# Expert rows added to token rows by indirect transfers, semaphores cleared inside other stages, slabs stored by partition

## The chip, the cores and the metric

The kernel runs on one NeuronCore of a Trainium2 chip, as one program. The metric is the device time of one execution in microseconds (us). The core's engines are PE (TensorE, matrix products and transposes), DVE (VectorE), ACT (ScalarE), POOL (GpSimd) and SP (SyncE, which only issues transfers and waits); PEld is the loading of weights into PE. Transfers between DRAM and the on-chip memory are issued from the queues of SP, ACT and POOL and are carried out by 16 DMA engines that all queues share.

## What is computed

Two blocks, each a graph convolution followed by a feed-forward part, on x of 16 items x 512 nodes x 16 channels x 12 times. Seen as tokens, an item is 192 rows (one per channel and time) of 512 values, so there are 3072 token rows.

```python
x = x + L0_conv(ln_c(x))
t = to_tokens(x);  t = t + L0_ffn(ln_t(t));  x = from_tokens(t)   # mixture of experts
x = x + L1_conv(ln_c(x))
t = to_tokens(x);  t = t + L1_ffn(ln_t(t));  x = from_tokens(t)   # ternary weights, 8-bit activations

def L0_ffn(x):                       # E = 8 experts, cap = 1.25 * N * 2 / E = 960 rows each
    gate = softmax(x @ Wr.T)         # N = 3072 token rows of H = 512
    top2_val, top2_idx = top_k(gate, 2)
    # first choices of all tokens, then second choices, are ranked within their expert;
    # an assignment ranked over cap gets weight 0
    y_e = (silu(x @ Wg[e].T) * (x @ Wu[e].T)) @ Wd[e].T
    return sum_e comb[:, e] * y_e    # comb: the kept gate values
```

## The kernel before, in words

The program is a row of stages. Each stage is one block of code in which every engine has its own instruction stream; engines are ordered by semaphores (a wait is `wait_ge(sem, value)`), and at the end of a block all engines meet before the next block begins. Nothing of a stage overlaps the next one. The stages in order are: constants; `normalise` n0 (layer norm of x over nodes, item by item); `conv_weights`; the channel attention c0; `mix_channels`; the time attention t0; `graph_conv` g0, which writes x1; `normalise` n1, which also keeps the unnormalised token rows in DRAM (`raw_rows`) and computes the router's logits; `route`; `experts`; `combine`; `conv_weights`, c1, mixing, t1 and `graph_conv` g1 of the second block; `quantise_weights`; `feed_forward`.

Item order inside a stage is software pipelined by hand: `turns` calls `turn(b, q, i)` for each item b with q = b mod 2 naming the buffer, and one turn holds parts of item b, b+1 and b+2 (`third`, `second`, `first`). `ready(n)` and `free(n, depth)` are the semaphore values for "n is done" and "the buffer that n will use is free".

**Slabs.** x, x1, x2 and x3 lie in DRAM as [item, node, channel x time]; a slab of an item is loaded into 128 partitions of 4 x 192 values, that is 512 runs of 768 bytes.

**Semaphores.** Each stage makes its own. `Semaphores.clear` sets all that were made since the last call back to zero in a block of its own, by one SP instruction each (L119), and frees them. It is called after g0 and after `quantise_weights`.

**route** finds for each token its two experts and its place (slot) in each. Slot numbers go into `s.slots`, gate values into `s.gates`, and a table of which token sits in each of 64 tiles of 120 slots is made by products of one-hot matrices on PE (L1073) and two DVE steps (L1149, L1150).

**experts** handles 8 experts of 8 tiles of 120 rows. POOL gathers the rows of the tiles ahead (`x_xin`, L1221), PE transposes them (`ex_t`), and PE computes gate and up products (`ex_g`, `ex_u`) and the down product (`ex_d`), each as three passes of high and low parts. ACT copies `ex_d` out of PSUM (`x_yo`, L1396, two buffers) and stores it to `y_slots` in DRAM (L1398).

**combine** ("join") then goes item by item: SP loads the raw rows (L1459), POOL gathers four times 96 rows of `y_slots` (L1482; two halves of an item x two choices), DVE adds the four with their gate values (L1506), takes statistics (L1522, L1523 and the four small steps of `node_stats`, L254 to L260), POOL raises to the power -0.5 (L1488), DVE makes the shift `L_nm` (L266), ACT normalises into `L_xnT` (L1580) and copies `L_xa` out of PSUM (L1570), PE transposes both (L1544), DVE copies the transposed rows into `L_shared` (L1529), SP stores `xn_rows`, ACT stores x2 (L1573). Raw rows have two buffers. At its start ACT's queue issues the 13 loads of the next convolution's weights (`conv_loads`, L167).

## Time and profile before

| what | value |
|---|---|
| runs shown | 1921.21, 1924.47 and 3712.32 us; median 1924.47 us |
| profiled execution, its own time | 1922.03 us |
| its span, first to last instruction | 1920.2 us |
| busy shares of the span | PE 75%, DVE 61%, ACT 39%, POOL 28% |
| mean granted TensorE clock | 0.854 of full |
| DRAM traffic | 192.4 MB, mean 100 GB/s |

Reading it: the span is what the trace covers; 1.8 us of the execution lie outside it. The third run is nearly double the other two and is left out of every comparison below. Since the stages follow one another with a meeting of all engines between them, the shares of the whole say little: each stage has its own limit, and the time of the kernel is the sum of the stages'. By the first and last instructions of each in the trace, the long ones are g0 and g1 (313 us and 315 us), experts (434 us), feed_forward (258 us), combine (148 us), n1 (94 us), n0 (86 us) and route (59 us); c1 takes 15 us.

### The profile page before, as it was taken

Reading aid. Unit: us, or ns where it says so; the run is one execution under the profiler, and the core shown is the slowest. Engines: PE = TensorE matmul, PEld = TensorE weight load, DVE = VectorE, ACT = ScalarE, POOL = GpSimd, SP = SyncE. Lnnn points to the kernel's source line nnn. Section 1 sums busy time; section 2 is a strip of 40 time slices with the busy share of each in tenths; the row PEclk is TensorE's granted clock in tenths of the full one; section 3 lists DMA queues with packets and bytes.
Section 4 is the critical chain, followed back from the end, with each engine's and each line's share of the span. In section 5 each row is a group of like instructions: output and inputs, shape, how many; then the busy total and the mean of one; then the engine's idle time right before and its main releaser. Section 6 shows DMA issues by size and latency. Waiting matters only on the chain. (4 is left out here: it accounts for less than half of the span.)

```text
span 1920.2 us, 28801 instructions
## 1 busy us (share of the span) xinstructions
PE 1432.1 (75%) x8462; PEld 1174.9 (61%) x8462; DVE 1163.3 (61%) x2466; ACT 746.6 (39%) x1181; POOL 532.3 (28%) x854
## 2 busy tenths in 40 slices
PE   4577999997462499999999533487999994177776
PEld 3466788886241388888888423385888883145554
DVE  4622588887366555444444267522688886588886
ACT  2412455553241133333333122222555552077765
POOL 1100155566111311111110256200255665011111
PEclk7678999998696599999999755587999997588988
DMA  6432022222472133344441587343122221112221
GB/s 194 139 89 76 17 67 73 61 70 66 140 229 84 46 113 115 120 121 122 127 127 42 157 241 243 118 132 121 35 73 60 71 74 49 34 57 74 83 89 58
DMA packets 152117, 192.42 MB, mean 100 GB/s; under 512 B 11737, under 2 KB 103417, under 8 KB 152061
## 3 DMA queue, kind: packets, MB, share of 16 engines
q1 hardware_dynamic: 118061, 129.16, 22.7%
q10 hardware_dynamic: 24784, 34.24, 6.0%
q0 software_dynamic: 9216, 28.32, 4.9%
q8 instruction: 29, 0.48, 0.1%
q14 instruction: 27, 0.22, 0.0%
HBM read 125.63 MB, written 66.06 MB: 100 GB/s over the span
## 5 line engine op out<-in xcount | busy, mean ns | idle before, releaser
L724 PE MATMUL g_y<-L_z,L_pt 128*128 128x192 f32 x1024 | 195.8, 335 | 1.5 <-ACT L_pt L937 0.5
L724 PEld LDWEIGHTS g_y<-L_z,L_pt 128*128 128x128 f32 x1024 | 165.6, 192 | 6.8 <-ACT L_pt L937 6.8
L882 POOL TENSOR_TENSOR L_xr<-L_xr,L_lnb 128x192 f32<-128x192 f32 x128 | 105.6, 853 | 204.5 <-DMA L_xr<-x 108.5
L1221 POOL DMA_INDIRECT x_xin<-xn_rows,x_index x64 | 64.2, 1003 | 298.2 <-PE ex_t L1235 150.5
L929 ACT ACTIVATE L_e<-g_s,L_nm 128x512 f32<-128x512 f32 x128 | 88.0, 687 | 78.7 <-DVE L_nm L770 77.5
L692 PE MATMUL g_z<-L_kw,L_xnT 96*128 96x192 f32 x512 | 96.8, 344 | 26.1 <-DVE L_v L800 26.1
L692 PEld LDWEIGHTS g_z<-L_kw,L_xnT 96*128 96x128 f32 x512 | 87.1, 198 | 38.2 <-DVE L_v L800 38.2
L1315 DVE TENSOR_TENSOR x_mid<-ex_g,x_sig 128x480 f32<-128x480 f32 (+1 forms) x48 | 31.4, 654 | 122.5 <-ACT x_sig L1390 122.5
L770 DVE TENSOR_REDUCE L_nm<-g_s 128x1 f32<-128x512 f32 x128 | 87.5, 684 | 25.4 <-PE g_s L701 24.6
L779 DVE SCALAR_TENSOR_TENSOR L_p<-L_e,L_rl,L_adj 128x512 f32<-128x512 f32 x128 | 99.1, 774 | 4.7 <-DVE L_rl L777 0.3
L1368 ACT ACTIVATE x_xh<-ex_t 128x480 fp32r<-128x480 f32 x64 | 36.6, 572 | 160.1 <-PE ex_t L1235 151.8
L937 ACT ACTIVATE L_pt<-g_t 128x512 f32<-128x512 f32 x128 | 75.8, 593 | 45.6 <-PE g_t L709 45.4
L889 POOL TENSOR_TENSOR L_t<-L_rstd 128x48 f32<-128x48 f32 x96 | 29.2, 304 | 222.4 <-DVE L_rstd L824 217.3
L709 PE MATMUL g_t<-s_ident,L_p 128*128 128x128 f32 x512 | 77.4, 274 | 9.6 <-DVE L_p L779 9.6
L1745 PE MATMUL ff_u<-s_wup,ff_q1s 128*96 128x512 bf16 x256 | 79.0, 464 | 5.4 <-DVE ff_q1s L1830 4.0
L899 POOL TENSOR_TENSOR L_d<-L_d,L_lng 128x192 f32<-128x192 f32 x128 | 73.1, 602 | 35.7 <-DVE L_d L830 35.7
L709 PEld LDWEIGHTS g_t<-s_ident,L_p 128*128 128x128 f32 x512 | 63.2, 140 | 30.4 <-DVE L_p L779 25.2
L720 PEld LDWEIGHTS g_y<-L_res,L_xnT 97*128 97x128 f32 x512 | 75.4, 193 | 6.2 <-ACT L_y L943 1.1
L1249 PE MATMUL ex_g<-x_xh,x_guh 128*128 128x480 f32 (+1 forms) x192 | 76.9, 400 | 3.1 <-DVE x_gul L1306 3.1
L320 PE MATMUL n_psx<-s_ident,L_xa 128*96 128x128 f32 x256 | 45.3, 338 | 43.4 <-DMA L_xa<-x 28.7
L1263 PE MATMUL ex_d<-x_wdh,x_hh 128*120 128x512 f32 (+1 forms) x192 | 77.7, 404 | 0.0
L720 PE MATMUL g_y<-L_res,L_xnT 97*128 97x96 f32 x512 | 75.5, 270 | 0.5 <-ACT L_y L943 0.5
(273 smaller groups left out, 3791.9 us busy)
## 6 DMA issues: line engine op xcount, KB each, us to landing
xn_rows<-L_xnT SPq DMA_DIRECT2D x48, 384.0 KB, 3.7
L_xnT<-xn_rows SPq DMA_DIRECT2D x48, 384.0 KB, 3.4
y_slots<-x_yo ACTq DMA_DIRECT2D x64, 240.0 KB, 2.4
x<-L_y SPq DMA_DIRECT2D x32, 384.0 KB, 2.7
L_xa<-in_x SPq DMA_DIRECT2D x16, 384.0 KB, 4.0
L_raw<-xn_rows SPq DMA_DIRECT2D x16, 384.0 KB, 3.4
L_xr<-in_x SPq DMA_DIRECT2D x16, 384.0 KB, 3.8
L_xa<-x SPq DMA_DIRECT2D x16, 384.0 KB, 4.1
```

Source lines behind the costliest of these rows:

```text
L692: last = nc.tensor.matmul(psz[:, k // 2, CT * (k % 2):CT * (k % 2) + CT], xnT[q][0:HALF, h, P * k:P * k + P], kw[q][0:HALF, h, NPROJ:], st ...
L709: last = nc.tensor.transpose(pst[k % 2][:, P * c:P * c + P], pr[k % 2][:, P * c:P * c + P], s.ident[:, :])
L720: nc.tensor.matmul(out[:, HALF * h:HALF * h + HALF], xnT[q][0:HALF + 1, h, P * k:P * k + P], s.res[0:HALF + 1, h, :], start=(h == 0), stop ...
L724: last = nc.tensor.matmul(out, pt[k % 2][:, P * c:P * c + P], z[q][:, c, :], start=False, stop=(c == NK - 1))
L770: nc.vector.tensor_reduce(s.nm2[:, k % 2:k % 2 + 1], pss[k % 2][:, :], AX, ALU.max, negate=True).then_inc(nmax_done, 1)
L779: nc.vector.scalar_tensor_tensor(out=pr[k % 2][:, :], in0=e[k % 2][:, :], scalar=s.rl[:, k % 2:k % 2 + 1], in1=s.adj[:, k, :], op0=ALU.mul ...
L882: last = nc.gpsimd.tensor_tensor(v_, v_, gain(s.lnb), ALU.add)
L929: nc.scalar.activation(e[k % 2][:, :], pss[k % 2][:, :], ACT.Exp, bias=s.nm2[:, k % 2:k % 2 + 1], accum_out=s.l[:, k % 2:k % 2 + 1]).then_ ...
L937: nc.scalar.activation(pt[k % 2][:, :], pst[k % 2][:, :], ACT.Copy).then_inc(probs_turned_sb, 1)
L1249: last = nc.tensor.matmul(ps_[z][0:size, 0:SN], w[:, k, off + at:off + at + size], x[q][:, k, SN * c:SN * c + SN], start=(k == 0 and x is ...
L1263: last = nc.tensor.matmul(psd[t % 2][0:ST, :], h[0:size, j, ST * t:ST * t + ST], w[0:size, j, :], start=(j == 0 and h is hh and w is wdh), ...
L1745: last = nc.tensor.matmul(psu[0:HALF, c, :], q1s[q][:, k, HALF * h:HALF * h + HALF], wup[:, k, 512 * c:512 * c + 512], start=(k == 0), sto ...
```

## The change

Four things change.

1. **Expert rows are added in DRAM.** `raw_rows` becomes the first 3072 rows of a tensor `sums`, with 960 spare rows behind them. `experts` multiplies a tile by its gate values while it leaves PSUM (ACT, scale from `x_gate`), and POOL adds it into `sums` with an indirect transfer whose destination rows come from a table and which adds to what is there. Unused slots go to spare rows. The gate values are gathered by POOL, 120 values of 4 bytes per tile, from a small DRAM tensor `gate_rows` that `route` writes. Output tiles get four buffers in place of two. An expert's additions start only when all of the expert before have landed. `y_slots`, `s.slots`, the gathers of `combine` and its weighted sums are gone.
2. **combine is written anew** around loads of `sums`: raw rows have four buffers, all four are loaded at the start, and SP issues the stores of x2 as well.
3. **Semaphores are cleared inside other stages**: by SP in `experts` (those of the stages before it) and in the attention c1. The two blocks of `clear` are gone.
4. **Slabs are stored by partition**: x, x1, x2, x3 lie as [item, partition, 4 x 192], one run of 3072 bytes per partition. The host lays x out so; the output keeps the old form.

`route` also makes two more tables (where a slot's gate value lies, and to which row it is added), with a third block of columns in the one-hot product.

Of the diff stand here the new parts and what they replace; the removed gathers and weighted sums of `combine` are those of the function above.

```diff
-    def clear(self):
-        with self.nc.Block() as block:
-            @block.sync
-            def _(sp):
-                for sem in self.live:
-                    sp.sem_clear(sem)
-        self.ctx.close()
-        self.live = []
+    def retire(self):
+        self.old, self.retired, self.live, self.ctx = self.live, self.ctx, [], ExitStack()
+    def clear_retired(self, sp):
+        for sem in self.old:
+            sp.sem_clear(sem)
+    def reuse(self):
+        self.retired.close()
...
+                if clear:
+                    s.sems.clear_retired(sp)
...
+                sp.wait_ge(gated, 2)
+                for c in range(2):
+                    at = TOKENS * (c + 1)
+                    sp.dma_start(gate_rows[at:at + TOKENS, :].rearrange("(p j) o -> p (j o)", j=TILES),
+                                 s.gates[:, c, :]).then_inc(gates_out, 16)
+                sp.wait_ge(gates_out, 32)
...
+                for c in range(2):
+                    act.wait_ge(hots, 2 * c + 1)
+                    nc.scalar.activation(col_tok[c][:, :, 2, :], col_hot[c][:, :, :], ACT.Copy,
+                                         scale=float(c + 1)).then_inc(hots_kind, 1)
...
-                        last = nc.tensor.matmul(pst[0:ST, 0:2 * ST_TILES], row_hot[c][:, j, :],
+                        last = nc.tensor.matmul(pst[0:ST, 0:3 * ST_TILES], row_hot[c][:, j, :],
...
-                step(V.tensor_copy(low[:, :], pst[0:ST, 0:ST_TILES]))
-                V.scalar_tensor_tensor(out=s.table[:, :], in0=pst[0:ST, ST_TILES:2 * ST_TILES], scalar=float(TOKEN_BASE),
-                                       in1=low[:, :], op0=ALU.mult, op1=ALU.add).then_inc(tabled, 1)
-                dve.wait_ge(tabled, 1)
+                step(V.tensor_copy(made[:, :], pst[0:ST, 0:3 * ST_TILES]))
+                part, tile, kind = (made[:, ST_TILES * n:ST_TILES * n + ST_TILES] for n in range(3))
+                step(V.scalar_tensor_tensor(out=token[:, :], in0=tile, scalar=float(HALF), in1=part,
+                                            op0=ALU.mult, op1=ALU.add))
+                V.tensor_copy(s.table[:, 0, :], token[:, :]).then_inc(tabled, 1)
+                step(V.scalar_tensor_tensor(out=gate_at[:, :], in0=part, scalar=float(TILES), in1=tile,
+                                            op0=ALU.mult, op1=ALU.add))
+                V.scalar_tensor_tensor(out=s.table[:, 1, :], in0=kind, scalar=float(TOKENS), in1=gate_at[:, :],
+                                       op0=ALU.mult, op1=ALU.add).then_inc(tabled, 1)
+                step(V.scalar_tensor_tensor(out=spare[:, :], in0=kind, scalar=0.0, in1=spare[:, :],
+                                            op0=ALU.is_equal, op1=ALU.mult))
+                V.tensor_tensor(s.table[:, 2, :], token[:, :], spare[:, :], ALU.add).then_inc(tabled, 1)
+                dve.wait_ge(tabled, 3)
...
+                s.sems.clear_retired(sp)
...
+                def gather(e, ts):
+                    pool.wait_ge(index_done, ready(e))
+                    for t in ts:
+                        n = e * EST + t
+                        if n >= 4:
+                            pool.wait_ge(turned, ready(n - 4))
+                        nc.gpsimd.indirect_dma_start(xin[t % 4][:, :], None, tokens,
+                                                     row(index[e % 2][:, t:t + 1])).then_inc(x_in[t % 4], 16)
+                def gather_gates(e):
+                    pool.wait_ge(places_done, ready(e))
+                    for t in range(EST):
+                        nc.gpsimd.indirect_dma_start(gate[e % 2][:, t:t + 1], None, gate_rows,
+                                                     row(places[e % 2][:, 0, t:t + 1])).then_inc(gates_in, 16)
+                def scatter(e, ts):
+                    if ts is early and e > 0:
+                        for j in range(4):
+                            pool.wait_ge(sent[j], scattered(e))
+                    for t in ts:
+                        pool.wait_ge(y_sb, ready(e * EST + t))
+                        nc.gpsimd.indirect_dma_start(sums, row(places[e % 2][:, 1, t:t + 1]), yo[t % 4][:, :], None,
+                                                     compute_op=ALU.add).then_inc(sent[t % 4], 16)
+                early, late = range(EST // 2), range(EST // 2, EST)
+                gather(0, early)
+                gather(0, late)
+                gather(1, early)
+                for e in range(E):
+                    gather_gates(e)
+                    if e + 1 < E:
+                        gather(e + 1, late)
+                    scatter(e, early)
+                    if e + 2 < E:
+                        gather(e + 2, early)
+                    scatter(e, late)
+                for j in range(4):
+                    pool.wait_ge(sent[j], scattered(E))
...
+                            if n == 3 and ahead:
+                                for j in range(4) if reused else ():
+                                    dve.wait_ge(sent[j], scattered(e))
+                                copy_places(e + 1, r)
...
-                def send(e, t):
+                def send(e, q, t, reused):
                     n = e * EST + t
+                    if t == 0:
+                        act.wait_ge(gates_in, (e + 1) * (16 * EST))
                     act.wait_ge(down_done, ready(n))
-                    act.wait_ge(sent[t % 2], dma_free(e * (EST // 2) + t // 2))
-                    nc.scalar.activation(yo[t % 2][:, :], psd[t % 2][0:ST, :], ACT.Copy).then_inc(y_sb, 1)
-                    act.wait_ge(y_sb, ready(n))
-                    act.dma_start(ys[n], yo[t % 2][:, :]).then_inc(sent[t % 2], 16)
-                def turn(e, q, here=True, ahead=True):
+                    if reused or t >= 4:
+                        act.wait_ge(sent[t % 4], scattered(e) + t // 4 * 16)
+                    nc.scalar.activation(yo[t % 4][:, :], psd[t % 2][0:ST, :], ACT.Identity,
+                                         scale=gate[q][:, t:t + 1]).then_inc(y_sb, 1)
...
+        raw = [(half(s.raw0, 0), half(s.raw0, 1)), (half(s.raw1, 0), half(s.raw1, 1)),
+               (s.e0[0:HALF, :], s.e1[0:HALF, :]), (s.p0[0:HALF, :], s.p1[0:HALF, :])]
+        xnT, x2 = [s.xnT0, s.xnT1], [s.xa0, s.xa1]
...
+                def load(b, z):
+                    sp.wait_ge(xn_done, free(b, 4))
+                    sp.wait_ge(raw_turned, free(b, 4))
+                    for h in range(2):
+                        sp.dma_start(raw[z][h], raw_rows[b][:, h, :]).then_inc(row_in[z], 16)
+                def store(b, r):
+                    sp.wait_ge(xn_done, ready(b))
+                    sp.dma_start(xn_rows[b], xnT[r][0:HALF, :, :]).then_inc(sent[r], 16)
+                    sp.wait_ge(x_sb, ready(b))
+                    sp.dma_start(x_nodes[b], x2[r][:, :, :]).then_inc(kept[r], 16)
+                for b in range(4):
+                    load(b, b)
+                store(0, 0)
+                store(1, 1)
+                with sp.Fori(0, B // 4 - 1) as i:
+                    for z in range(4):
+                        load(i * 4 + z + 4, z)
+                        store(i * 4 + z + 2, z % 2)
+                store(B - 2, 0)
+                store(B - 1, 1)
...
+                def statistics(b, z, i):
+                    step.begin(b * STAT_STEPS)
+                    dve.wait_ge(row_in[z], (i + 1) * 32)
+                    nc.vector.bn_stats(s.bst[0:HALF, 0, :], raw[z][0])
+                    step(nc.vector.bn_stats(s.bst[0:HALF, 1, :], raw[z][1]))
+                    node_stats(nc, s, step, z % 2, eps).then_inc(var_done, 1)
...
+                def apply_norm(b, z, stores):
+                    r = z % 2
+                    act.wait_ge(shift_done, ready(b))
+                    act.wait_ge(back_turned, free(b, 2))
+                    act.wait_ge(sent[r], stores * 16)
+                    for h in range(2):
+                        last = nc.scalar.activation(half(xnT[r], h), raw[z][h], ACT.Identity,
+                                                    bias=s.nm[0:HALF, r, h:h + 1], scale=s.rs[0:HALF, r, h:h + 1])
+                    last.then_inc(xn_done, 1)
+                def copy_x(b, z, stores):
+                    r = z % 2
+                    act.wait_ge(raw_turned, ready(b))
+                    act.wait_ge(kept[r], stores * 16)
+                    nc.scalar.activation(x2[r][:, :, :].rearrange("p (a k) x -> p a (k x)", a=2),
+                                         psx[r][:, :, 0:2 * CT], ACT.Copy).then_inc(x_sb, 1)
...
+    by_partition = lambda a: a.rearrange("b p (k x) -> b p k x", k=NK)
...
-    xn_rows, raw_rows = dram("xn_rows", [TOKENS, N]), dram("raw_rows", [TOKENS, N])
-    x1, x2, x3 = (dram(n, [B, N, CT]) for n in ("x1", "x2", "x3"))
-    y_slots = dram("y_slots", [SLOTS + 1, N])
+    xn_rows, sums = dram("xn_rows", [TOKENS, N]), dram("sums", [TOKENS + EST * ST, N])
+    raw_rows = sums[0:TOKENS, :]
+    x1, x2, x3 = (dram(n, [B, P, NK * CT]) for n in ("x1", "x2", "x3"))
+    gate_rows = dram("gate_rows", [3 * TOKENS, 1])
...
-            s.sems.clear()
-            normalise(nc, s, "n1", node_major(x1), 1e-5, rows(xn_rows), keep=rows(raw_rows))
+            graph_conv(nc, s, "g0", rows(xn_rows), by_partition(d["x"]), by_partition(x1))
...
+                s.sems.retire()
+                small_attention(nc, s, "c1", True, clear=True)
+                s.sems.reuse()
+                (ternary,) = s.sems("loads2", "ternary")
...
-            s.sems.clear()
-            feed_forward(nc, s, node_major(x3), node_major(out))
+            feed_forward(nc, s, by_partition(x3), node_major(out))
...
-    d["x"] = a["x"].transpose(0, 1, 3, 2).reshape(B, N, CT)
+    slabs = a["x"].transpose(0, 1, 3, 2).reshape(B, NK, P, CT)
+    d["x"] = slabs.transpose(0, 2, 1, 3).reshape(B, P, NK * CT)
```

How the change moves instructions, at three places.

**SP, from the end of g0 into n1.** Before: `L_y` is the last slab of g0, the row at L119 is the clearing.

```order
L622 DMA L_xr<-in_x 128x4x192
L626 DMA x<-L_y 128x4x192 x2
L608 UNCONDITIONAL_BRANCH
L116 UNCONDITIONAL_BRANCH
L119 ISA x83
L115 UNCONDITIONAL_BRANCH
L288 UNCONDITIONAL_BRANCH
L297 DMA L_xa<-x 128x4x192 x2
```

The same place of the changed kernel:

```order
L629 DMA L_xr<-in_x 128x768
L633 DMA x<-L_y 128x768 x2
L615 UNCONDITIONAL_BRANCH
L290 UNCONDITIONAL_BRANCH
L299 DMA L_xa<-x 128x768 x2
L242 UNCONDITIONAL_BRANCH
```

The block with 83 clearings is gone; the loads of n1 follow the last stores with one block boundary between.

**POOL, experts.** Before, a loop over pairs of experts whose body is 16 of these gathers, each behind a step of a register; its beginning:

```order
L1027 UNCONDITIONAL_BRANCH
L1206 UNCONDITIONAL_BRANCH
L1213 UNCONDITIONAL_BRANCH
L1215 ISA
L1221 DMA x_xin<-xn_rows,x_index 120x512
L1217 REGISTER_ALU
```

The changed kernel, from the start of the stage to the second expert's additions (`x_gate` gate values, `sums` the additions of `x_yo`):

```order
L1244 UNCONDITIONAL_BRANCH
L1254 DMA x_xin<-xn_rows,x_index 120x512 x12
L1260 DMA x_gate<-gate_rows,x_places 120x1 x8
L1254 DMA x_xin<-xn_rows,x_index 120x512 x4
L1269 DMA sums<-x_yo,x_places 4032x512 x4
L1254 DMA x_xin<-xn_rows,x_index 120x512 x4
L1269 DMA sums<-x_yo,x_places 4032x512 x4
L1260 DMA x_gate<-gate_rows,x_places 120x1 x8
L1254 DMA x_xin<-xn_rows,x_index 120x512 x4
```

Per expert POOL now issues 8 gathers of rows, 8 of gate values and 8 additions, where it issued 8 gathers of rows.

**DVE, combine, one item.** Before, first item (the loop's turns hold the same, with the copies of `cb_wgt` and `cb_idx` behind):

```order
L1506 SCALAR_TENSOR_TENSOR L_raw<-L_e,cb_wgt,L_raw 96x512
L1506 SCALAR_TENSOR_TENSOR L_raw<-L_p,cb_wgt,L_raw 96x512
L1506 SCALAR_TENSOR_TENSOR L_raw<-L_e,cb_wgt,L_raw 96x512
L1506 SCALAR_TENSOR_TENSOR L_raw<-L_p,cb_wgt,L_raw 96x512
L1522 BN_STATS L_bst<-L_raw 96x6
L1523 BN_STATS L_bst<-L_raw 96x6
L254 TENSOR_TENSOR L_mv<-L_bst 96x4
L255 TENSOR_TENSOR L_dm<-L_bst 96x2
L256 SCALAR_TENSOR_TENSOR L_dm<-L_dm 96x2
L258 SCALAR_TENSOR_TENSOR L_dm<-L_mv,L_dm 96x2
L260 TENSOR_SCALAR L_vt<-L_dm 96x2
L266 SCALAR_TENSOR_TENSOR L_nm<-L_mv,L_rs 96x2
```

The changed kernel, its third and fourth item:

```order
L1582 COPY L_shared<-join_a 128x768
L268 SCALAR_TENSOR_TENSOR L_nm<-L_mv,L_rs 96x2
L1576 BN_STATS L_bst<-L_p 96x6
L1577 BN_STATS L_bst<-L_p 96x6
L256 TENSOR_TENSOR L_mv<-L_bst 96x4
L257 TENSOR_TENSOR L_dm<-L_bst 96x2
L258 SCALAR_TENSOR_TENSOR L_dm<-L_dm 96x2
L260 SCALAR_TENSOR_TENSOR L_dm<-L_mv,L_dm 96x2
L262 TENSOR_SCALAR L_vt<-L_dm 96x2
L1582 COPY L_shared<-join_a 128x768
L268 SCALAR_TENSOR_TENSOR L_nm<-L_mv,L_rs 96x2
```

The four weighted sums ahead of the statistics are gone, and the shift `L_nm` of an item stands behind the statistics of the next item and the copy of the item before, where it stood directly behind its own statistics.

## Rows read from the trace of the kernel before

**Rows 1.** Busy time of each engine in three stretches: n1, experts, combine.
```profile
core 0: us, PE busy (x) PEld busy (x) DVE busy (x) ACT busy (x) POOL busy (x), PEclk, DMA share, GB/s
495.00:590.00 95.00, 58.33 (x391) 38.48 (x392) 53.33 (x160) 39.32 (x48) 10.99 (x16) 0.88 0.69 199
648.00:1082.00 434.00, 418.68 (x1984) 339.57 (x1984) 196.02 (x320) 140.65 (x235) 64.22 (x64) 0.97 0.37 108
1082.00:1231.00 149.00, 49.28 (x256) 39.97 (x256) 97.19 (x242) 35.38 (x48) 78.07 (x80) 0.50 0.76 231
```

**Rows 2.** The clearing instructions, and the timeline around both blocks of clearing (start us, us).
```profile
L119 SPq EVENT_SEMAPHORE_RANGE_CLEAR  x224: 25/30/49, 490.0 to 1661.6; - x112
...
486.96 0.38 SPq L626 DMA_DIRECT2D x<-L_y  x1
495.76 5.92 SPq L297 DMA_DIRECT2D L_xa<-x  x3
...
1652.82 0.06 DVE L1629 MEMSET s_minus_magic<- 128x2 f32 x1
1662.21 0.38 SPq L1692 DMA_DIRECT2D ff_xa<-x  x1
```

**Rows 3.** Timeline of one item in the middle of combine.
```profile
1150.19 0.16 DVE L266 SCALAR_TENSOR_TENSOR L_nm<-L_mv,L_rs 96x2 f32<-96x2 f32 x1 [0.92 <-POOL L_rs L1488]
1150.32 0.96 DVE L1529 COPY L_shared<-join_a 128x768 f32 x1
1150.47 1.52 ACT L1580 ACTIVATE L_xnT<-L_raw,L_nm,L_rs 96x512 f32<-96x512 f32 x2 [6.04 <-DVE L_nm L266]
...
1152.12 1.54 PE L1544 MATMUL join_a<-s_ident,L_xnT 96*128 96x96 f32 x8 [3.41 <-ACT L_xnT L1580]
...
1152.44 0.75 DVE L1506 SCALAR_TENSOR_TENSOR L_raw<-L_pt,cb_wgt,L_raw 96x512 f32<-96x512 f32 x1 [1.02 <-DMA L_z<-y_slots,cb_idx]
...
1155.33 0.69 DVE L1522 BATCH_NORM_STATS2 L_bst<-L_raw 96x6 f32<-96x512 f32 x1
...
1157.63 0.72 POOL L1488 TENSOR_TENSOR L_rs<-L_vt,s_mhalf 96x2 f32<-96x2 f32 x1 [0.31 <-DVE L_vt L260]
```

**Rows 4.** Timeline: last store of experts, last early load, and the end of combine.
```profile
1079.53 0.34 ACTq L1398 DMA_DIRECT2D y_slots<-x_yo  x1
...
1088.54 1.75 ACTq L167 DMA_DIRECT2D L_xnT<-in_k_ones  x2
...
1224.20 0.16 DVE L266 SCALAR_TENSOR_TENSOR L_nm<-L_mv,L_rs 96x2 f32<-96x2 f32 x1 [0.80 <-POOL L_rs L1488]
...
1230.83 0.19 DVE L194 TENSOR_SCALAR L_wm<-L_wm 96x60 f32<-96x60 f32 x1 [2.32 <-PEq L1445]
```

**Rows 5.** Timeline: the eight transposes of one item in n1.
```profile
542.47 0.88 PE L337 MATMUL n_psa<-s_ident,L_xnT 96*128 96x96 f32 x8
```

**Rows 6.** POOL's gathers: busy, mean ns, idle before (one expert, 750 to 801.3 us); ns min/median/max (all).
```profile
L1221 POOL DMA_INDIRECT x_xin<-xn_rows,x_index x8 | 7.9, 984 | 43.4 <-PE ex_t L1235 22.2 <-DVE x_index L1289 20.4 <-issue 0.9
...
L1221 POOL DMA_INDIRECT x_xin<-xn_rows,x_index x64: 980/984/1472, 650.3 to 1002.9; - x64
```

**Rows 7.** The page's list of transfers: count, KB each, median us from issue to landing.
```profile
L_xnT<-xn_rows SPq DMA_DIRECT2D x48, 384.0 KB, 3.4
y_slots<-x_yo ACTq DMA_DIRECT2D x64, 240.0 KB, 2.4
x<-L_y SPq DMA_DIRECT2D x32, 384.0 KB, 2.7
...
L_xa<-in_x SPq DMA_DIRECT2D x16, 384.0 KB, 4.0
...
x_xin<-xn_rows,x_index POOLq DMA_INDIRECT x64, 3.9
```

**Rows 8.** Timeline: the end of route.
```profile
643.71 3.67 PE L1073 MATMUL rt_table<-r_col_tok,r_row_hot 96*120 96x128 bf16 x32 [15.64 <-DVE r_col_tok L1145]
647.41 0.22 DVE L1149 COPY r_low<-rt_table 120x64 f32<-120x64 f32 x1 [3.76 <-PE rt_table L1073]
```

**Rows 9.** Waits of the whole span (us in total, times, longest), the row of n0's slabs.
```profile
PE n_psx L320 <- DMA L_xa<-in_x: 14.7, 8, 11.6
```

276 lines of the change are left out of this document (111 added, 165 removed).

## The prediction

> **What bounds the kernel now.** I read the busy times by stage first, because all engines meet between stages: what a change is worth is read inside its stage, and the stages add up. In experts PE is busy for 418.7 of 434 us at a granted clock of 0.97, while DVE, ACT and POOL are below half [rows 1]: that stage is PE's, and nothing on another engine costs time there until it holds PE up. Combine is the opposite: in 149 us DVE is busy for 97, POOL for 78, PE for 49, ACT for 35, so no engine bounds it alone; it is a chain through all of them [rows 1]. The timeline of one item shows the chain: DVE waits 1.02 us for a gather to land, spends four steps of about 0.75 us on the weighted sums (1152.44 to the statistics at 1155.33), 2.3 us on the statistics until POOL starts at 1157.63, then comes POOL's 0.72, and ACT's two normalisations 1.52 [rows 3]. Over the stage that is (1230.83 - 1082.5) / 16 = 9.3 us per item. The rest of the change touches places where every engine stands still: the two blocks of clearing [rows 2], and the end of route [rows 8].
>
> **Clearing.** The second gap runs from the last memset's end (1652.88) to the first load of feed_forward (1662.21): 9.33 us with 141 clearings. The first runs from the last store's landing (486.96 + 2.7 us, [rows 7]) to 495.76: 6.1 us with 83. The difference, 3.2 us for 58, gives 0.056 us each, and leaves 1.45 us that does not depend on their number, two block boundaries and the first steps of the next stage [rows 2]. All 224 go off the path: 12.5 us, and with each block one of two boundaries, for which I take a third of the 1.45, together 1.0. Sum -13.5 us; between -12.5 and -15. What hides them now: 100 stand on SP behind the last weight load of experts, 5.6 us in a stage where SP is free for its last 50 us, and 63 in c1, 3.5 us of a stage of 15 us with no other work on SP. Without that cover they would cost what they cost now.
>
> **Combine.** The new stage has no gathers and no sums, and I work out its period anew. DVE's order is statistics of item b, copy of b-2, shift of b-1. The shift lets ACT normalise b-1, then PE transposes it, and DVE needs that for its copy of b-1, behind which stands the next shift. That is a closed circle: copy 0.96, shift 0.16, handover to ACT 0.12 (from 1150.35 to 1150.47), normalise 1.52, handover 0.13 (1151.99 to 1152.12), transposes 1.54, and two handovers of about 0.05: 4.5 us [rows 3]. The transposes are at the lower clock level (granted 0.50 in this stage); at the upper one eight of them took 0.88 us [rows 1, 5], and the circle is 3.8 us. PE will be denser than now (two times 1.54 in 4.5 us), so some items should see the upper level; I take 4.4. What else could be longer: DVE's own work is 0.96 + 0.16 + 2.3 = 3.4; ACT's 1.52 and a copy of three quarters of the columns, 1.1, is 2.6; PE's 3.1; SP issues four transfers of about 0.4 us [rows 2]. The DMA engines carry three transfers of 384 KB, 1.18 MB per item. They moved 231 GB/s at a busy share of 0.76 here, so at most about 304 GB/s with such packets: 3.9 us per item. That is close under 4.4, so the loads will land later than their 3.4 us [rows 7], but four buffers let SP ask for a row about six us before DVE needs it.
> The start: the first rows land about 4.3 us in, two statistics and POOL's step follow, so the first shift comes at 8.8 us, just when ACT is through with its 13 early loads (1088.54 + 1.75 is 7.8 us after the stage began) [rows 4]. Then 15 periods of 4.4, 66 us, and the tail from the last shift to the next stage, 6.6 us now (1224.20 to 1230.83) and built alike. Sum 81.4 us against 148.3: -66.9 us. With 3.8 us per item it is -76; with the 5.2 us that n1 takes per item for the same traffic and a similar circle (94 us for 16 items, less its start and end) it is -55.
>
> **Experts, inside.** POOL now has 24 indirect transfers per expert where it had 8. A gather costs 0.98 us and 0.30 of idle behind it [rows 6]: 24 x 1.28 = 30.7 us in an expert of 51.3 us (7.9 busy + 43.4 idle, [rows 6]). No row shows an adding transfer or one of 4-byte rows. From below their price is the 0.98, from above I put the longest gather, 1.47: 8 x 1.28 + 16 x 1.77 = 38.6 us, still 12.7 us short. The order on POOL also fits. The first four additions of an expert are issued as its tiles leave PSUM, then four gathers (5.1 us) for the expert after next, whose first tile PE wants some 5 us into the next expert, then four additions, eight gate gathers and the last gathers. ACT's wait for a buffer: tile 4 needs the addition of tile 0 landed, four tiles later, and PE has one more tile of room. A tile is nine products of 0.21 us (418.7 us for 1984, [rows 1]), so that is about 10 us. A gather lands in 3.9 us [rows 7]. DVE's new wait, ahead of `copy_places` in the middle of an expert, holds the shifts of the hidden products behind it, and through them PE; it comes 72 products or 15 us into an expert, some 10 us after the last of the additions it waits for is issued. ACT's scaling in place of its copy costs at most 0.76 us a tile, half of a pair of normalisations [rows 3], and lies under PE. I put all of this at 0, with up to +10 us.
> **Experts, end.** The last tile goes to DRAM by a store issued at 1079.53 that lands after 2.4 us [rows 4, 7]. Now POOL has to be told, and its transfer lands after 3.9 us if it is like a gather; an addition must read before it writes, for which I add 1.5, and 0.3 for ACT and the handover. +3.3 us, between +1.5 and +8 (the longest landing I allow is twice the median).
>
> **Route.** The product of the second choices is 32 matrix products that took 3.67 us with 128 columns; with 192 they take half as much again if columns set their pace, +1.8 us, and nothing if the weight loads do [rows 8]. Then DVE has seven small steps where it had two of 0.22 us, five more at about 0.26 with their waits: +1.3. One more constant is loaded ahead of the one that DVE waits for: +0.45. Two casts fall away: -0.4. The third column block is made on ACT beside POOL's, and the gate values are stored long before the stage ends: 0. Sum +3.2, between +1 and +5.
>
> **Slabs by partition.** A slab's load in 512 runs of 768 bytes lands after 4.0 us, rows in runs of 2048 bytes after 3.4 [rows 7]. So a load may gain 0.6 us. In n0 PE waits for slabs 8 times for 14.7 us, and 11.6 of it is the first [rows 9]: the other 3.1 us are short waits, each ahead of a wait for statistics, so I count only the starts: n0, n1 and feed_forward, -0.3 us each, -1 together; at most -5.
> The Trainium skill (DMA: Bandwidth & Descriptors, "Why small descriptors are slow") puts the loss of small descriptors to a fixed overhead of a few cycles per packet. By that a run of 768 bytes loses about a tenth of its moving time, some 0.1 us of a landing of 4.0, and the three starts would give -0.3 in place of -1. The rows differ by more than that, and I go by them.
>
> **Sum.** 1922.0 (the profiled execution) - 13.5 - 66.9 + 0 + 3.3 + 3.2 - 1 = 1847.1 us. The profiled execution lies 2.4 us under the median of the runs shown, 1924.47, and equals their lower end; I say 1848. A measurement of this kernel can tell about 2% from no change, 38 us, and the forecast is 4% down.
>
> **Rivals.**
> *Combine held by its transfers.* The 304 GB/s are an extrapolation; at a share near 0.95 each load and store waits for others, and the stores of `L_xnT`, which two items later must be free, come into the circle. Against it: at 4.4 us the need is 268 GB/s. For it: n1 moves the same and takes 5.2. Price 15 x 0.8 = +12 us: 1860.
> *Combine and the loads faster.* PE at the upper level throughout (3.8 us per item, -9) and slabs worth -3 more: 1836.
> *POOL becomes the bound of experts, and the kernel ends slower.* If an addition or a gate gather costs p in place of 1.28 us, POOL needs 10.3 + 16 p per expert; from p = 2.56 us PE waits for gathered rows, 16 us for every further us of p in each of 8 experts. To lose the 77 us that the rest gains p must be 3.2; at 3.5 it is 8 x (10.3 + 56 - 51.3) = +120 us: 1968. For it: no row shows such transfers, and the longest gather took half as long again as the median [rows 6]. Against it: beside a DVE that is busy 45% of the stage [rows 1] the 64 gathers have a median of 0.984 and a minimum of 0.980, so hardly one was disturbed [rows 6].
> The Trainium skill (SBUF — State Buffer, "Who interferes with whom") says that DVE in its two-port modes blocks GpSimd, and so the writing of descriptors for its transfers, for a whole instruction. That speaks against moving work to this queue. If each of the 16 new transfers lost a whole DVE copy of 0.96 us [rows 3], POOL would need 10.3 + 16 x 2.24 = 46 us, still under 51.3; so the rule raises this rival's chance and doesn't make it the forecast.
> *The additions land slowly.* Each expert's wait for all of the one before, a landing over some 10 us: with 15 us +5 us per expert, +40: 1888, no change.
> That the change doesn't take the clearing off the path is excluded by the order of instructions.
>
> **Chances.** Forecast 0.70, transfers in combine 0.12, faster 0.10, slow additions 0.04, POOL bound 0.04. The range takes in the first three with the bounds of experts' end and inside: 1829 (clearing -15, combine -76, route and end at their low ends, slabs -5) to 1876 (combine -55, end +8, route +5, some 8 inside experts). Faster by over 2% 0.91, within 2% 0.05, slower 0.04.
>
> **What would show it.** Combine about 81 us long, DVE's copy, shift, ACT and PE in a circle of 4.4 us. PE in experts busy without gaps, POOL at some 31 us per expert. No idle stretch of more than about 4 us around 490 us and before feed_forward. Route about 62 us. It would be wrong if additions cost over 2.5 us on POOL or land after over 10 us, or if combine's loads come late.

## The result

The changed kernel takes 1863.41 us (median of 4 runs, 1862.13 to 1866.03). The kernel before took 1920.07, 1921.21, 1924.47 and 3712.32 us beside it; without the last, which stays out of the comparison, the median is 1921.21 us (with it 1922.84). The ratio is 0.970, 95% interval 0.968 to 0.971: faster by 3.0%, some 58 us. The forecast was 1848 us, 74 us under the profiled execution of before; the time lies within its range, 1829 to 1876, and 3 us from the 1860 of the rival "combine held by its transfers".

The profiled execution took 1862.88 us, span 1861.1. By stage, each from its first to its last instruction in the two traces (us; the first row is the sum of the two gaps between stages, in front of n1 and of feed_forward):

```
stage                     before    after   change   forecast
clearing, both gaps         14.2      0.0    -14.2     -13.5
combine                    148.4     95.3    -53.1     -66.9
experts                    434.1    441.9     +7.8      +3.3
route                       58.7     60.75    +2.0      +3.2
n0                          86.0     83.8     -2.1   } -1.0 for
feed_forward               258.4    257.1     -1.3   } slabs
g0                         312.8    314.6     +1.8       0
all others together                           ~0         0
```

### The profile page after: what moved, and what is told of

The parts are those of the page before. It is cut to its first block and busy times, and to the rows that moved or that the text cites. A ratio compares the mean times of both kernels' runs of the same rounds, so it can differ in the third digit from the quotient of the medians.

```text
span 1861.1 us, 28248 instructions
## 1 busy us (share of the span) xinstructions
PE 1435.1 (77%) x8462; PEld 1179.6 (63%) x8462; DVE 1113.9 (60%) x2381; ACT 751.4 (40%) x1181; POOL 635.8 (34%) x918
## 5 line engine op out<-in xcount | busy, mean ns | idle before, releaser
L1269 POOL DMA_INDIRECT sums<-x_yo,x_places x64 | 103.0, 1609 | 136.4 <-ACT x_yo L1472 126.3
L1441 ACT ACTIVATE x_xh<-ex_t 128x480 fp32r<-128x480 f32 x64 | 36.5, 570 | 109.3 <-PE ex_t L1297 92.2
L1981 POOL TENSOR_TENSOR ff_yo<-ff_ya,ff_xr 128x768 f32<-128x768 f32 x16 | 29.6, 1852 | 139.0 <-DVE ff_ya L1935 139.0
```

Of the source, the lines that this page charges most:

```text
L1269: nc.gpsimd.indirect_dma_start(sums, row(places[e % 2][:, 1, t:t + 1]), yo[t % 4][:, :], None, compute_op=ALU.add).then_inc(sent[t % 4], 16)
```

## The profile after

Busy time of each engine in n1, experts and combine, to be read beside [rows 1]:

```profile
490.10:584.40 94.30, 58.06 (x384) 38.14 (x384) 53.32 (x160) 39.37 (x48) 11.00 (x16) 0.88 0.67 200
645.20:1087.10 441.90, 418.61 (x1984) 339.27 (x1984) 195.89 (x328) 141.35 (x233) 234.50 (x192) 0.96 0.52 106
1087.10:1182.40 95.30, 46.09 (x256) 40.30 (x256) 47.59 (x144) 35.39 (x48) 11.02 (x16) 0.50 0.71 230
```

In experts PE is busy for 418.6 us, as before, though POOL went from 64 to 234 us, and an expert takes 51.3 us from its first product to that of the next, as before: nothing inside the stage holds PE. With 0.30 us of idle behind each of 24 transfers, POOL is taken for some 36.5 us of each expert. In combine DVE's and POOL's work has halved or more, and yet no engine is busy for over half of the 95 us: it is still a chain. The kinds of POOL's transfers in experts:

```profile
L1269 POOL DMA_INDIRECT sums<-x_yo,x_places x64 | 103.0, 1609 | 136.4 <-ACT x_yo L1472 126.3 <-issue 10.1
L1260 POOL DMA_INDIRECT x_gate<-gate_rows,x_places x64 | 66.7, 1043 | 19.5 <-issue 19.5
L1254 POOL DMA_INDIRECT x_xin<-xn_rows,x_index x64 | 64.8, 1012 | 51.2 <-DVE x_index L1351 18.6 <-issue 16.4 <-PE ex_t L1297 14.0
```

An addition takes 1.61 us, 0.6 more than a gather [rows 6], a gather of 4-byte rows 1.04.

The timeline of one item in the middle of combine, beside [rows 3]:

```profile
1140.29 0.35 SPq L1538 DMA_DIRECT2D xn_rows<-L_xnT  x1
1140.32 1.54 PE L1605 MATMUL join_a<-s_ident,L_xnT 96*128 96x96 f32 x8 [1.73 <-ACT L_xnT L1634]
1140.99 0.37 SPq L1540 DMA_DIRECT2D x<-L_xa  x1
1141.61 1.35 SPq L1534 DMA_DIRECT2D L_p<-sums  x2
1141.67 0.69 DVE L1576 BATCH_NORM_STATS2 L_bst<-L_e 96x6 f32<-96x512 f32 x1 [3.11 <-DMA L_e<-sums]
...
1143.75 0.96 DVE L1582 COPY L_shared<-join_a 128x768 f32 x1
...
1144.62 0.15 DVE L268 SCALAR_TENSOR_TENSOR L_nm<-L_mv,L_rs 96x2 f32<-96x2 f32 x1
1144.81 1.52 ACT L1634 ACTIVATE L_xnT<-L_raw,L_nm,L_rs 96x512 f32<-96x512 f32 x2 [3.84 <-DVE L_nm L268]
...
1147.28 0.69 DVE L1576 BATCH_NORM_STATS2 L_bst<-L_p 96x6 f32<-96x512 f32 x1 [2.51 <-DMA L_p<-sums]
```

The rows into `L_p` are asked for at 1141.61, in two transfers, and DVE can begin on them at 1147.28, 5.7 us later. Before both items DVE stands still for a DMA (3.11 and 2.51 us); the copy, which the forecast had as a link of the circle, starts with no wait. The first shift comes at 1095.93, the last at 1175.97: 8.8 us of start, 15 periods of 5.34, 6.4 of tail. The forecast was 8.8 + 15 x 4.4 + 6.6. Only the period is off.

The rows also show which circle has this period. SP issues the store of a normalised item at 1140.29 and asks for rows at 1141.61; DVE begins on them at 1147.28; their statistics and the next copy start 2.1 us apart (copy at 1149.36); copy, shift and normalisation lead to the store of 1152.19. That is 1.3 + 5.7 + 2.1 + 2.8 = 11.9 us for two items here, and on average over the stage two items took 10.7.

What ends experts, from the instructions of the stage's block boundary (min/median/max ns, first and last start), of the changed kernel:

```profile
L1235 ACTq DRAIN  x1: 717/717/717, 1074.6 to 1074.6; - x1
L1235 POOLq COMPARE_BRANCH  x1: 41/41/41, 1081.2 to 1081.2; - x1
L1235 POOLq DRAIN  x1: 5490/5490/5490, 1081.4 to 1081.4; - x1
L1235 SPq EVENT_SEMAPHORE  x1: 17/17/17, 1087.1 to 1087.1; - x1
```

and of the kernel before:

```profile
L1198 POOLq DRAIN  x1: 6532/6532/6532, 1002.8 to 1002.8; - x1
L1198 ACTq DRAIN  x1: 14/14/14, 1082.2 to 1082.2; - x1
```

The last addition is issued at 1075.62, and POOL is through its wait for it at 1081.2: 5.5 us. Then POOL's queue drains for 5.49 us, and all engines wait for that. Before, POOL's drain took 6.53 us too, but at 1002.8, 79 us ahead of the end, where nobody saw it.

Route's end, beside [rows 8]:

```profile
L1095 PE MATMUL rt_table<-r_col_tok,r_row_hot 96*120 96x192 bf16 x32 | 5.2, 360 | 14.0 <-DVE r_col_tok L1165 14.0
```

5.2 us where it was 3.67, with half as many columns again: +1.5. The DVE steps behind it end 1.7 us after it, before 0.5. DVE's first wait, for the constant `r_tokens`, ends 5.3 us into the stage in both traces, and from there to the product it is 48.2 us where it was 48.9.

## Experiments

Ratios are to the kernel before, run on the same chip as each experiment; the changed kernel's own is 0.970. Times in us are medians.

**1. Clearing in blocks of its own again.**

```
+            s.sems.clear()
             normalise(nc, s, "n1", ...)
...
-            s.sems.retire()
...
-                s.sems.clear_retired(sp)
...
-                small_attention(nc, s, "c1", True, clear=True)
+                small_attention(nc, s, "c1", True)
...
+            s.sems.clear()
             feed_forward(nc, s, ...)
```

> The changed kernel with the two clearing blocks put back where they stood before (after the first graph_conv and before feed_forward), and no clearing inside experts and c1; all else as changed. The gaps of the two places were 5.5 and 8.7 us shorter in the changed kernel's trace, and experts ends with POOL, not with SP, so its clearings are hidden. Theory: +14 us, about 1877.5 us, with experts and c1 as long as in the changed kernel. Rival: the clearings inside experts or c1 cost there what they save elsewhere, then the sum is +8 us or less, and experts or c1 gets shorter.

1876.13 us, ratio 0.977 (0.975 to 0.979): 13.5 us slower than the changed kernel by the ratios. Experts took 441.9 us as before the edit, c1 15.2 (it varies between 14.7 and 16.6 over the traces). The two gaps were back at 5.5 and 8.8 us, and feed_forward, which is not touched, at 258.5. The clearings are hidden where they now stand, and their price was as forecast. Feed_forward's 1.3 us seem to belong to this part as well and not to the slabs: it takes 256.8 to 257.1 us in nine of the ten kernels without the two blocks, that of experiment 4 among them, but 259.7 in that of experiment 9. By what path the block ahead of it could cost feed_forward time, no run shows.

**2. Combine's rows asked for one item sooner.**

```
-                store(0, 0)
-                store(1, 1)
                 with sp.Fori(0, B // 4 - 1) as i:
                     for z in range(4):
+                        store(i * 4 + z, z % 2)
                         load(i * 4 + z + 4, z)
-                        store(i * 4 + z + 2, z % 2)
-                store(B - 2, 0)
-                store(B - 1, 1)
+                for b in range(B - 4, B):
+                    store(b, b % 2)
```

> The changed kernel with one thing moved: in combine SP asks for row b+4 right behind the stores of b, in place of behind the stores of b+1, so one item of about five us sooner. Theory one, late asking: in the changed kernel a row was asked for at 1141.61 and DVE began its statistics at 1147.28, 5.7 us later, and waited 2.5 us for it; the period was 5.34 us from (1175.97 - 1095.93) / 15. Asked for one item sooner the rows are there, the period falls to the circle of DVE, ACT and PE, 4.2 us in the last items which wait for no row, to 4.5: combine 81 to 84 us in place of 95.3, the kernel 1849 to 1852 us. Theory two, the DMA engines hold combine (rows and stores move 1.18 MB per item, 221 GB/s at 5.34 us): asking sooner only makes the rows land later, the period stays at 5.2 to 5.4 us, the kernel within 2 us of 1863.

1852.70 us, ratio 0.964 (0.962 to 0.965). Combine took 82.8 us; the first shift came at 1095.15, the last at 1163.57, a period of 4.56. The whole window of combine, and two rows of its waits (us, times, longest):

```profile
1087.10:1169.90 82.80, 45.59 (x256) 40.38 (x256) 47.20 (x144) 35.39 (x48) 11.01 (x16) 0.50 0.82 264
...
DVE L_bst L1574 <- DMA L_raw<-sums: 33.8, 2, 31.1
...
DVE L_shared L1580 <- PE join_a L1603: 23.0, 15, 3.3
```

In the changed kernel the rows read

```profile
DVE L_bst L1576 <- DMA L_raw<-sums: 45.6, 7, 32.1
...
DVE L_shared L1582 <- PE join_a L1605: 10.1, 5, 3.3
DVE L_bst L1576 <- DMA L_e<-sums: 9.0, 3, 3.5
DVE L_bst L1576 <- DMA L_p<-sums: 5.8, 3, 2.5
```

The same bytes, the same buffers and the work of every engine as it was, only SP's order changed: 12.5 us of combine hung on where SP asks. The circle through the request now spans three items, 4.0 us each by the rows above (an estimate), and is under the other. The waits for rows are gone but for the first and two of 2.7 and 1.6 us, and DVE now waits for PE's transposes 15 times, at its copy, which is the circle of the forecast. The granted clock is 0.50 in either kernel, so no item saw the upper level that the forecast hoped for; its circle at the lower level was 4.5 us. The engines' transfers did not hold the 5.34 us: they moved 264 GB/s here against 230.

**3. The wait for the last additions on SP.**

```
                 s.sems.clear_retired(sp)
+                for j in range(4):
+                    sp.wait_ge(sent[j], scattered(E))
...
-                for j in range(4):
-                    pool.wait_ge(sent[j], scattered(E))
```

> The changed kernel with the wait for the last additions, at the end of experts, moved from POOL to SP. In the changed kernel the last addition is issued at 1075.62, POOL passes its wait at 1081.2 and only then begins a DRAIN of 5.49 us, which ends the stage at 1087.1. Theory one: the drain has a length of its own and need not follow the landing, so it starts at 1077.3 and ends at about 1082.8, after the landing at 1081.2: experts 4.2 us shorter, the kernel 1859 us. Theory two: the drain waits for the indirect transfers themselves, about 5.5 us behind the last one's landing, and ends at 1087 all the same: no change.

1862.88 us, ratio 0.969 (0.967 to 0.972): no difference that the times can tell. The trace shows the stage at 440.0 us, 1.9 shorter, with these boundary rows:

```profile
L1235 POOLq DRAIN  x1: 9509/9509/9509, 1074.5 to 1074.5; - x1
L1235 SPq DRAIN  x1: 7/7/7, 1080.5 to 1080.5; - x1
```

Neither theory holds. The drain now begins at the issue of the last addition (1074.76) and ends at 1084.0, 3.8 us after the landing that SP saw at 1080.3, and not 5.5 us after POOL's last instruction (1076.35). So 3.8 us of drain follow the landing here and 5.5 in the changed kernel. What the drain waits for these times do not tell: over the kernels of this document it took between 4.3 and 7.5 us where it began behind the landing.

**4. Slabs by node.**

```
-    x1, x2, x3 = (dram(n, [B, P, NK * CT]) ...
+    x1, x2, x3 = (dram(n, [B, N, CT]) ...
...
-            normalise(nc, s, "n0", by_partition(d["x"]), ...
+            normalise(nc, s, "n0", node_major(d["x"]), ...
```

(and so at each use)

> The changed kernel with the slabs back in node order in DRAM (runs of 768 bytes in place of 3072 on the slab side), all else as changed. From the stages of the two traces: n0 was 2.1 us shorter with slabs by partition, feed_forward 1.3, n1 and combine could not be told apart, graph_conv was 1.8 us longer. Theory one, slabs by partition are worth the starts of the stages and nothing more: +1 to +4 us, about 1866. Theory two, they relieve combine, which waits for its transfers: its stores of the slab are short runs again, its rows land later, and combine alone gets 3 us or more longer, the kernel 1868 us or more.

1867.03 us, ratio 0.971 (0.969 to 0.973). By stage: n0 86.1 us in place of 83.8, combine 97.1 in place of 95.3, n1, g0 and feed_forward within 0.2 of the changed kernel. The ratios differ by 2 us, with some 4 of uncertainty; the stages add up to 4. It lies between the two theories: beside n0 it is combine that gains, by 1.8 us, less than the 3 that the second asked for. The n0 part is clear: the kernels with slabs by partition have 83.4 to 84.3 us. The combine part is weaker: where its code is that of the changed kernel, and with slabs by partition, it took between 94.6 and 96.0 us.

In n0 the first wait for a slab is as long in either (11.7 and 11.5 us), and the later items keep the same rhythm, shifts 4.0 and 5.5 us apart in turn, but for one interval of the changed kernel. The gain lies at the third item, whose slab PE has to wait for with runs of 768 bytes:

```profile
22.71 1.94 PE L322 MATMUL n_psx<-s_ident,L_xa 128*96 128x128 f32 x8 [1.21 <-DMA L_xa<-in_x]
```

and not with runs of 3072:

```profile
21.09 1.91 PE L322 MATMUL n_psx<-s_ident,L_xa 128*96 128x128 f32 x8
```

The second and third shift are 7.74 us apart in the first case and 6.29 in the second, which is 1.45 of the 2.2 us. Slab loads land 0.2 to 0.5 us sooner with the long runs (medians, for instance 4.2 and 3.9 us in n0, 3.9 and 3.4 in g0); nearly everywhere that hides behind other work.

**5. Both moves.** Edits 2 and 3 together.

> The changed kernel with two moves at once: rows of combine asked for one item sooner, and the wait for the last additions on SP. Alone the first gave a combine of 82.8 us in place of 95.3 and the second an experts stage of 440.0 us in place of 441.9, in their traces. They lie in different stages. Theory: they add up, 14 us under the changed kernel, a ratio to the kernel before of 0.9625, some 1850 us. Rival: what the second gives is lost again in the first steps of combine, which are held by ACT's early loads until 9.4 us into the stage: then 1852.

1848.55 us, ratio 0.961 (0.960 to 0.963). Experts 440.1, combine 82.3 us: their gains add up.

**6. The shift ahead of the copy.** On top of both moves, in DVE's turn of combine:

```
+                    if second:
+                        minus_mean(nc, s, dve, rstd_done, shift_done, b - 1, (z + 1) % 2)
                     if third:
                         copy_nodes(b - 2, z % 2)
-                    if second:
-                        minus_mean(nc, s, dve, rstd_done, shift_done, b - 1, (z + 1) % 2)
```

> The same as the kernel with both moves, and in combine DVE computes the shift of item b-1 ahead of its copy of item b-2, in place of behind it. With rows asked for sooner the period was (1163.57 - 1095.15) / 15 = 4.56 us. Theory one, the circle of my forecast (normalise, transposes, copy, shift, back to normalise) sets it: the copy is taken out of the circle, DVE's own work of 3.4 us, PE's two times 1.54 and ACT's 1.52 + 0.79 allow less, and the period falls to 3.9 to 4.1 us, where the transfers would hold it: combine 74 to 76 us, the kernel 1841 to 1843 us. Theory two, at 264 GB/s the transfers already set the 4.56 us: DVE waits for rows again and combine stays within 2 us of 82.8.

1840.75 us, ratio 0.957 (0.956 to 0.958), the fastest of all kernels here, 24 us under the changed one by the ratios and 7.8 under that of experiment 5 by the medians. (Its profiled execution took 1835.09, so its trace flatters the stages outside combine.) Combine took 73.0 us, its window and the waits that matter:

```profile
1081.40:1154.40 73.00, 45.69 (x256) 40.34 (x256) 48.01 (x144) 35.40 (x48) 11.01 (x16) 0.50 0.90 300
...
1100.00:1140.00 40.00, 29.40 (x169) 26.20 (x167) 31.14 (x92) 22.79 (x31) 6.86 (x10) 0.50 0.94 315
...
DVE L_bst L1574 <- DMA L_raw<-sums: 35.6, 5, 29.2
...
ACT L_xnT L1632 <- DMA xn_rows<-L_xnT: 6.2, 3, 3.1
...
SPq L1538 <- ACT L_xnT L1632: 18.6, 8, 5.8
```

The period is (1145.85 - 1089.36) / 15 = 3.77 us; the last interval is 1.0 us, the other 14 average 3.96. So the 4.56 us before was the circle through DVE's copy. With the copy out of it the transfers come close to being the limit: the DMA engines' share is 0.94 in the 40 us of the second row, DVE waits for rows again, and ACT waits three times for stores of `L_xnT` to land, a wait that the forecast's rival named and that the changed kernel did not have. The forecast's floor of 3.9 us, extrapolated from a busy share of 0.76 [rows 1], holds within 0.15 (at 315 GB/s it would be 3.75). One rival stands untested: SP issues all these transfers, and it waits for ACT ahead of only 8 of the 16 stores, where in the changed kernel it waited ahead of all 16, 48.0 us in all. Whether the transfers or the one queue that issues them hold the period, no run separates.

**7. Three gathers of gate values for each.** Two more indirect transfers behind each of `gather_gates`, into a tile `more`, counted on the same semaphore.

```
+                        for k in range(2):
+                            nc.gpsimd.indirect_dma_start(more[e % 2][:, k, t:t + 1], None, gate_rows,
+                                                         row(places[e % 2][:, 0, t:t + 1])).then_inc(gates_in, 16)
```

> The changed kernel with every indirect gather of gate values issued three times (the two extra ones into a tile that nobody reads), so 40 indirect transfers per expert on POOL in place of 24. In the changed kernel POOL is busy for 234.5 us in experts, 29.3 per expert, and stands idle 0.3 us behind each transfer: 36 of some 52.3 us. Theory, POOL can take more until its sum reaches an expert of PE: 16 more at 1.3 us make 57 us, 4.8 more than PE's 52.3, so experts gets about 38 us longer (30 to 50), the kernel 1901 us. Rival one: the transfers on this queue delay each other or PE's rows long before POOL is full, then much more than 50 us. Rival two: the extra ones hide in POOL's waits for tiles, under 15 us.

2003.66 us, ratio 1.042 (1.041 to 1.044), 139 us more than the changed kernel. The theory's 38 us and rival two's 15 are missed; rival one, much more than 50, holds, and it had no number of its own. POOL's sum would be 57 us per expert, but an expert took 68.2 us (five of PE's waits lie that far apart). What PE waits for:

```profile
PE ex_t L1301 <- DMA x_xin<-xn_rows,x_index: 84.6, 12, 15.0
```

Five of these waits are of 14.7 to 15.0 us; the other seven, 10.0 us together, belong to the first expert's start and stand in the changed kernel too. The five stand at the turn of the fifth row tile of the next expert. Take the first of them: the tile's gather is issued at 780.0, behind the last of 24 gate gathers, and PE turns the tile at 783.7. In the changed kernel the first of the four late gathers of rows is issued at 737.0 behind the gate gathers, lands about 741, and PE turns its tile at 746.3: 5.3 us in hand. 16 x 1.3 = 20.8 us more ahead of it, less 5.3, is 15.5 us. These five experts make 84 of the 139 us (68.2 for 51.3 us each); the rest lies in the first, 21 us, the seventh, 20, and the last, 12, where PE's gaps end with no releaser in the trace. POOL has 16 us per expert to spare as a sum and 5 in this place.

**8 and 9. Eight more gathers per expert, ahead of the late gathers or behind them.**

```
                     gather_gates(e)
+                    gather_more(e)      # 8: here
                     if e + 1 < E:
                         gather(e + 1, late)
+                    gather_more(e)      # 9: here instead
```

> The changed kernel with eight more indirect gathers of gate values per expert, into a tile that nobody reads, right behind the eight that are needed and so ahead of the four late gathers of rows. POOL then has 32 transfers per expert, some 36 + 10.4 = 47 us, under PE's 52.3. In the changed kernel's trace the first late gather is issued at 737.0, lands about 741, and PE turns its rows at 746.3: 5.3 us in hand. Theory one, a circle runs through that gather (the last tile's addition, gate gathers, late gathers, PE, the next expert's tiles): 10.4 - 5.3 = 5.1 us for each of seven experts, +36 us, about 1899 us. Theory two, POOL bounds experts only when its sum is longer than PE's (the forecast's rival): no change, within 3 us of 1863.

> The same eight extra gathers per expert, but issued behind the four late gathers of rows, where POOL otherwise waits from 743.3 until the next expert's first tile at 756.3, 13 us. Theory one (the circle through the late gathers): they take 10.4 of these 13 us and no PE work waits for them, no change, within 3 us of 1863. Theory two, it is the number of transfers on this queue that costs, wherever they stand: the same time as with the extra gathers ahead of the late ones.

Ahead: 1934.58 us, ratio 1.005 (1.004 to 1.007), experts 514.5 us. Behind: 1875.35 us, ratio 0.974 (0.971 to 0.978), experts 454.0. The place counts for 60 us with the same transfers, so theory two of both is out. But theory one gave 36 us for the first and got 72, and 0 for the second and got 12; and in the first PE waits for no row behind the first expert. (Behind, the 12 us are spread over all eight experts, 0.6 to 3.9 us each, and PE's gaps are 8.9 us longer in sum: at a tile turn in three experts, 1.2 to 1.3 us each, at a wait for ACT in two, and in short gaps without a releaser, most of them in the seventh expert, where the granted clock falls too.) The kernel with the gathers ahead shows something else, once in each of seven experts (windows from the one after the first, as [rows 1]):

```profile
750.00:754.00 4.00, 4.00 (x22) 3.48 (x21) 1.84 (x4) 0.57 (x1) 3.01 (x4) 1.00 0.83 279
754.00:760.00 6.00, 3.20 (x13) 1.96 (x11) 0.66 (x1) 0.57 (x1) 4.78 (x5) 1.00 0.02 0
760.00:766.00 6.00, 3.39 (x8) 2.10 (x8) 0.74 (x2) 0.79 (x2) 2.56 (x4) 0.56 0.43 123
766.00:770.00 4.00, 4.00 (x18) 3.13 (x17) 3.75 (x8) 0.82 (x3) 0.46 (x1) 0.80 0.21 64
```

PE takes 13 and 8 products in 6 us where at 0.21 us each it otherwise takes 28. Of its own groups between 754 and 765:

```profile
L1321 PE MATMUL ex_u<-x_xh,x_guh 128*128 128x480 f32 x4 | 1.9, 469 | 3.9 <-issue 3.9
```

The idle time ends with "issue": no semaphore that the profile shows. Six us later the granted clock falls to the lower level, and the products cost more until it is back. The seven experts with such a stretch are 8.8 to 12.6 us longer than in the changed kernel, 73 us together: this stretch, and not a wait for rows, is what the extra gathers ahead cost. The circle of experiment 7 is shown by its 15 us waits; for the smaller dose it was not what decided, since the stretches had already made each expert longer than the circle asked for.

**10. Writes in place of additions.** The sums are left out: a row of `sums` holds what was written to it last.

```
-                        nc.gpsimd.indirect_dma_start(sums, row(...), yo[t % 4][:, :], None,
-                                                     compute_op=ALU.add).then_inc(sent[t % 4], 16)
+                        nc.gpsimd.indirect_dma_start(sums, row(...), yo[t % 4][:, :], None).then_inc(sent[t % 4], 16)
```

> The changed kernel with the indirect additions of expert rows turned into indirect writes (the sums are left out: a row of sums holds the last row written to it), all transfers and waits as they are. In the changed kernel an addition takes POOL 1.60 us where a gather takes 1.0, and the last one is seen landed 5.5 us after its issue. Theory one: the addition itself costs, a write takes POOL 1.0 us and lands in 4.0 us, experts 1.5 us shorter, 1861.5 us. Theory two: it is the direction (SBUF to rows of DRAM) and not the addition, both numbers stay, no change. The drain of 5.49 us at the stage's end stays in either.

1907.52 us, ratio 0.992 (0.991 to 0.994): 43 us slower than with additions, which neither theory had. POOL's rows:

```profile
L1269 POOL DMA_INDIRECT sums<-x_yo,x_places x64 | 64.2, 1004 | 161.4 <-ACT x_yo L1471 154.1 <-issue 7.3
...
L1254 POOL DMA_INDIRECT x_xin<-xn_rows,x_index x64 | 63.9, 999 | 110.1 <-PE ex_t L1296 59.0 <-remote 19.6 <-DVE x_index L1350 18.6
```

On POOL theory one holds: 1.00 us for a write, 1.61 for an addition. The last one was seen landed after 3.3 us (issued 1117.55, wait passed 1120.8), the addition after 5.5. The drain, which was expected to keep its 5.49 us, took longer,

```profile
L1235 POOLq DRAIN  x1: 7491/7491/7491, 1121.1 to 1121.1; - x1
```

so that from the last issue to its end it is 11.0 us, with additions 11.3: the faster landing gave nothing at the stage's end. And inside the stage the kernel is slower, by stretches in six of the experts like the one above, which make these experts 57.3 to 58.7 us long in place of 51.3:

```profile
725.00:730.00 5.00, 5.00 (x26) 4.27 (x25) 1.92 (x3) 0.38 (x1) 3.85 (x4) 1.00 0.04 5
730.00:735.00 5.00, 2.64 (x13) 1.56 (x12) 0.66 (x1) 0.19 (x1) 3.93 (x4) 1.00 0.02 0
735.00:740.00 5.00, 3.69 (x9) 2.25 (x9) 1.98 (x4) 2.69 (x6) 0.98 (x1) 0.56 0.30 71
```

Here POOL issues eight gate gathers, as the changed kernel does, 2.6 us sooner after its tiles. In that kernel PE has no gap of over 0.15 us from 665 to 1074. Stretches of this kind stand in the first and the seventh expert of experiment 7 too. Three of them, one of each of experiments 7, 8 and 10, begin while POOL issues gathers of 4-byte rows and the DMA share is at 0.02. Whether the gathers make them, and by what path, no run here shows; it stays open. A rival that nobody tested is that PE lacks instructions, which the page of the profile lists as transfers too: one of the seven stretches of experiment 8 has such a packet in it, but the trace records too few of them to tell (none of queue 8 between 834 and 1106 us).

## Why the prediction was right or wrong

**Clearing** (-13.5): -14.2 in the gaps, 13.5 by experiment 1. The price of 0.056 us each and the cover in experts and c1 were right. Feed_forward's 1.3 us came with it unforeseen.

**Combine** (-66.9): -53.1. The step that failed is "four buffers let SP ask for a row about six us before DVE needs it". SP's order is store of b + 1, load of b + 4: the load of an item stands behind the store of the item three before it, so it is asked for some 1.3 us after that item is normalised, and DVE would be ready for it 2.9 us after that same point (transposes 1.54, copy 0.96, shift and handovers). That is 1.6 us of lead, and for the item shown 5.7 were needed: two transfers of 192 KB, the second issued 1.0 us after the first and landing 4.6 us later. The six us are what one more item gives, and with them (experiment 2) the stage is 82.8 us where the forecast said 81.4; start and tail, 8.1 and 6.3, and the circle, 4.56 for 4.4, were right (4.5 was its sum without the upper clock level, which never came). I had read how many buffers there are, and not behind which store each request stands in the queue. The forecast named the sign itself: it would be wrong if combine's loads came late. The landing beside other transfers was also taken too short, 3.4 us for a median of 3.8 to 4.1 and 4.6 in this case; the list of transfers of before had a row from this very stage,

```profile
L_raw<-raw_rows SPq DMA_DIRECT2D x16, 384.0 KB, 4.7
```

but the lead is what decides: with 3.4 us of landing it would still be short.

**Its rival** (1860) came out nearest, and that is luck: its mechanism, transfers that wait for each other at a high share, was not at work at 5.34 us, as experiment 2 shows. Signs of it appear in the kernel of experiment 6, at 3.77. That the forecast's own range held is in part luck too: combine missed by 13.8 us of a range of 47.

**Experts, inside** (0): right for this kernel, PE's busy time and gaps are the same; from the stage's start to PE's last product it is 429.5 us where it was 430.6. The bound for the new transfers, 0.98 to 1.47 us, was too low for the additions: 1.61. The landing of an addition, 3.9 + 1.5 = 5.4 by estimate, was 5.5.

**Experts, end** (+3.3): the stage is 7.8 us longer, and from PE's last product to its end it is 12.5 us where it was 3.5, +9.0. The term lacks POOL's drain: 5.5 us between the landing and the end of the block, hidden before because POOL was long done. Taking it away leaves +3.5, the forecast's term. Experiment 3 shows that 1.9 us of it can be had back by moving the wait.

**POOL as the bound** (0.04, 1968): the working was wrong though the case did not come up. It compared POOL's sum with PE's, 38.6 us against 51.3, and gave a threshold of 2.56 us for a transfer. Experiment 7 shows that 5.3 us is all that the late gathers have in hand, a threshold of 1.3 + 5.3 / 8 = 2.0 us for a gate gather. The kernels of experiments 8 and 10 lost 68 and 43 us in yet another way, by the stretches in PE, which neither working has; the second of them did so with less work on POOL than the changed kernel. The chance was too low for what the profile could tell. The delay by DVE that the forecast allowed for here, 0.96 us for each new transfer, did not come: beside a DVE that is busy for 44% of the stage the 64 additions took 1.59 to 1.66 us and the gathers of rows 1.01 in the mean. That is weak evidence on copies, though: DVE's work in experts is nearly all operations of two inputs, with casts of 0.43 us in between, and no copy like that one.

**Route** (+3.2): +2.0. The product +1.5 for +1.8 and DVE's steps +1.2 for +1.3 were right. The constant (+0.45) cost nothing, and the steps between it and the product are 0.66 shorter, where -0.4 was expected from the casts.

**Slabs** (-1): -2.2 in n0 by experiment 4's stages, and up to -1.8 in combine, which is not clear of its spread. Each load lands 0.2 to 0.5 us sooner, where 0.6 was taken. The mistake was to look at the first wait of a stage alone: in n0 it is as long as before, and most of the gain is PE's wait for the third slab, 1.2 us, one of the short waits that I had counted as hidden. n1 and feed_forward gained nothing that experiment 4 can tell.

**g0** is 1.8 us longer, with either form of slabs and with either form of clearing; I have no cause for it.

Together: 13.8 of combine, 4.5 of experts (the end's +9.0 less 1.1 inside) and 1.8 of g0, less 0.7, 1.2, 1.1 and 1.3 for the rest, is 15.8 us, the distance between the forecast's 1847.1 and the profiled execution's 1862.9.

## What to carry to other kernels

How early a buffered load is asked for is not set by the number of buffers but by what stands ahead of it in its queue: write down, for one item, which earlier item's store the request follows, and count from there to the consumer. When the last work of a stage moves to another engine, add what that engine needs to close its block, read from where it is now hidden. And an engine with time to spare in sum can be at its limit in one place: find the transfer that others wait for and measure its slack, not the engine's share. Even that slack does not price everything: two of the edits here lost 43 and 68 us by a slow PE whose cause stays open.

## What was not expected of the hardware

- In experts POOL's queue drained for 5.49 us after its indirect transfers though the last of them had landed before, and for 4.3 to 7.5 us in the kernels of experiments 7 to 10; begun earlier, it ended 3.8 us after the landing. In combine, where the changed kernel has no indirect transfer, POOL's drain took 0.65 us, before it took 6.04.
- An indirect addition of 120 rows of 2 KB cost POOL 1.61 us and was seen landed after 5.5; the same write without the addition 1.00 and 3.3.
- PE can slow to half or a quarter of its products for 6 to 12 us with no wait that the trace shows, followed by the lower clock level, and a change on another engine that only saves work there (writes for additions) brought this on and made the kernel 43 us slower.
